# Mixture of experts: fp32 weights cast to bf16 by GpSimd's operations, and by transfers that GpSimd issues

## The chip, the cores and the metric

The kernel runs on one core of a Trainium2 chip. The metric is the device time of one execution in microseconds; the figure given for a kernel is the median of its runs. One further execution is recorded by the hardware profiler, and all rows below are from that one.

## The reference

A decoder of four layers over a tensor `x` of 4 x 256 tokens with 256 channels. Each layer adds an attention-like block, a cross block and a feed-forward block. The change lies in the feed-forward block of the first layer, a mixture of 64 experts of which each token uses 8:

```
router_logits = x2d @ gate_w                       # 1024 x 64
routing_weights, selected = top_k(softmax(router_logits), 8)
routing_weights /= sum(routing_weights)
layer_w0 = ragged_dot(x_bf16, gate_proj_bf16)      # expert e: 256 x 96
layer_w1 = ragged_dot(x_bf16, up_proj_bf16)        # expert e: 256 x 96
expert_out = ragged_dot(silu(layer_w0) * layer_w1, down_proj_bf16)   # 96 x 256
out = sum over the 8 experts of routing_weight * expert_out, to bf16
```

The weights come in as fp32 (`gate_proj`, `up_proj`, `down_proj`) and are rounded to bf16 before the products.

## The kernel before

The whole decoder is one program of stages, one after the other, each ended by a barrier of all engines. The function `mixture` (L1099) is the stage at hand. It computes every expert for every token and multiplies by the routing weight, which is 0 where the expert was not chosen.

**Units of weights.** An expert has only 96 inner columns, and the engines have 128 rows. The host packs four experts into three units of 128: unit r of a group holds the 96 columns of expert r and 32 columns of the fourth expert. So there are U = 48 units (`MOE_N`) for 64 experts. A unit has an up part (`moe_up[i]`, 128 x 512 fp32, gate and up weights, 256 KB) and a down part (`moe_down[i]`, 128 x 256 fp32, 128 KB). I call the work of one group, three units and four experts, a turn; there are 16.

**Rings.** SP loads unit i into slot i % 6 of the fp32 rings `wf` and `df` (L1161, L1162; `MOE_RING` = 6) and waits before it for the cast of unit i - 6. The two transfers of a unit raise one semaphore `loads[i % 6]`. GpSimd (`cast_weights`, from L1166) waits for both, and then copies `wf` into the bf16 ring `wb` (6 slots, L1172) and `df` into the bf16 ring `db` (9 slots, L1173). Before it writes it waits until the slots are free: for `wb` until TensorE has done the up product of unit i - 6 (`u_done`), for `db` until the down products of the group that used the slot are done (`o_done`). This last wait is the same for the three units of a group, so the casts come in bursts of three units. GpSimd also clears the accumulator `acc` once (L1178), after the casts of the first two units.

**The other engines, by unit i.** TensorE computes the gate and the up product of unit i for 1024 tokens into PSUM (`pg`, `pu`, L1198), when unit i is cast and the previous contents were read, and then the down products of the experts completed by unit i - 3 (`po`, L1213, `LAG` = 3). ScalarE copies `pg` to bf16 (L1229), computes the sigmoid from exponentials and a logarithm (L1232, L1247, L1249), and copies each expert's output from PSUM into `eo` (L1240). VectorE copies `pu` (L1297), adds 1 to the exponential (L1300), adds each expert's output times its routing weight into `acc` (L1308, eight instructions of 128 x 256 for an expert), and multiplies (L1318, L1324). After units 2, 5, 8, ... of a group the fourth expert is complete too, so VectorE then has two experts in a row: 16 instructions of L1308. At the start VectorE also computes the routing (L1266 to L1287) in three parts between the first units; TensorE's router products (L1186) come ahead of its first unit.

**Order.** Each engine's instructions run in the order written; between engines there are only the semaphores named. SP has nothing in this stage but the loads.

Of the kernel before, what the change touches and what calls it, by code (L numbers as in the profile page):

```python
# [15 lines left out]
BF16 = mybir.dt.bfloat16  # L16
# [4 lines left out]
P = 128  # L21
B = 4
S = 256
D = 256
KT = D // P
# [1066 lines left out]

MOE_E, MOE_F, MOE_N, MOE_RING = 64, 96, 48, 6
MOE_BIG = 2.0 ** 63


def mixture(nc, g):  # L1099


    res, xT, I = g["res"], g["xT"], g["in"]
    TOK = B * S
    with Stage(nc, "moe") as wst:
        acc = wst.sbuf("acc", [P, NT, D])
        wsel = wst.sbuf("wsel", [P, NT, MOE_E])
        xb = wst.sbuf("xb", [P, KT, TOK], BF16)
        wf = wst.sbuf("wf", [P, MOE_RING, KT, 2, P])
        df = wst.sbuf("df", [P, MOE_RING, D])
        gate = wst.sbuf("gate", [P, KT, MOE_E])  # L1110
        loads = [nc.alloc_semaphore(f"moe_loaded{r}", num=SEM_MOE + r) for r in range(MOE_RING)]
        normalize(nc, g, [(gate[:, :, :], I["moe_gate"])])

        with Stage(nc, "moee") as st:
            R, H, U, LAG = MOE_RING, 9, MOE_N, 3
            LAST = MOE_E - 1

            def before(i):

                return 4 * (i // 3) + i % 3  # L1120

            def experts(i):

                return range(before(i), before(i + 1))

            def pieces(e):

                n, r = 3 * (e // 4), e % 4
                return [(n + r, slice(0, MOE_F))] if r < 3 else [(n + i, slice(MOE_F, P)) for i in range(3)]

            wb = st.sbuf("wb", [P, R, KT, 2, P], BF16)
            db = st.sbuf("db", [P, H, D], BF16)
            gb = st.sbuf("gb", [P, 4, TOK], BF16)
            ub = st.sbuf("ub", [P, 4, TOK], BF16)
            ex = st.sbuf("ex", [P, 4, TOK], BF16)
# [11 lines left out]
            pl = po[:, 0:2, :].rearrange("p a (t e) -> p (a t) e", e=MOE_E)  # L1147
            logits, v_chain, shifted, prob_done, xb_done, zeroed = st.sem(
                "logits", "v_chain", "shifted", "prob_done", "xb_done", "zeroed")
            (cast, g_done, u_done, g_read, u_read, exp_done, one_plus, ln_done, inv_done, gated, h_done,  # L1150
             o_done, o_read, used, summed, rounded) = st.sem(
                "cast", "g_done", "u_done", "g_read", "u_read", "exp_done", "one_plus", "ln_done",
                "inv_done", "gated", "h_done", "o_done", "o_read", "used", "summed", "rounded")
            with st.block() as block:

                @block.sync
                def _(sp):
                    for i in range(U):
                        if i >= R:
                            sp.wait_ge(cast, i - R + 1)  # L1160
                        sp.dma_start(wf[:, i % R, :, :, :], I["moe_up"][i]).then_inc(loads[i % R], 16)  # L1161
                        sp.dma_start(df[:, i % R, :], I["moe_down"][i]).then_inc(loads[i % R], 16)  # L1162

                @block.gpsimd
                def _(pool):
                    def cast_weights(i):  # L1166
                        pool.wait_ge(loads[i % R], 32 * (i // R + 1))
                        if i >= R:
                            pool.wait_ge(u_done, i - R + 1)
                        if i >= H:  # L1170
                            pool.wait_ge(o_done, 4 * before(3 * ((i - H) // 3 + 1)))
                        nc.gpsimd.tensor_copy(wb[:, i % R, :, :, :], wf[:, i % R, :, :, :])  # L1172
                        nc.gpsimd.tensor_copy(db[:, i % H, :], df[:, i % R, :]).then_inc(cast, 1)  # L1173

                    AHEAD = 2
                    for i in range(AHEAD):
                        cast_weights(i)
                    nc.gpsimd.memset(acc[:, :, :], 0.0).then_inc(zeroed, 1)  # L1178
                    for i in range(AHEAD, U):
                        cast_weights(i)  # L1180

                @block.tensor
                def _(pe):
                    for t in range(NT):
                        for k in range(KT):
                            last = nc.tensor.matmul(pl[:, t, :], xT[:, k, t // ST, (t % ST) * P:(t % ST + 1) * P],  # L1186
                                                    gate[:, k, :], start=(k == 0), stop=(k == KT - 1))
                    last.then_inc(logits, 1)
                    pe.wait_ge(xb_done, KT)
                    for i in range(U + LAG):  # L1190
                        if i < U:
                            pe.wait_ge(cast, i + 1)
                            for n, (ps, read, done) in enumerate(((pg, g_read, g_done), (pu, u_read, u_done))):
                                if i >= 1:
                                    pe.wait_ge(read, i)
                                for half in range(2):
                                    for k in range(KT):
                                        last = nc.tensor.matmul(  # L1198
                                            ps[:, half, :], wb[:, i % R, k, n, :],
                                            xb[:, k, half * 512:(half + 1) * 512], start=(k == 0), stop=(k == KT - 1))  # L1200
                                last.then_inc(done, 1)
                        if i >= LAG:
                            pe.wait_ge(h_done, i - LAG + 1)
                            for e in experts(i - LAG):
                                for q in range(4):
                                    if e >= 1:
                                        pe.wait_ge(o_read, 4 * (e - 1) + q + 1)
                                    elif q == 0:
                                        pe.wait_ge(shifted, 1)
                                    for t in range(2 * q, 2 * q + 2):  # L1210
                                        parts = pieces(e)
                                        for n, (j, rows) in enumerate(parts):
                                            last = nc.tensor.matmul(  # L1213
                                                po[:, t, :], hb[rows, j % H, t * P:(t + 1) * P], db[rows, j % H, :],
                                                start=(n == 0), stop=(n == len(parts) - 1))
                                    last.then_inc(o_done, 1)
# [336 lines left out]
def attend(nc, g, name, H, HD, NKV, causal, scale, qparts, kparts, stacks, vaug, w_out, b_out, carried):  # L1553
# [12 lines left out]
    LAG = H + 12  # L1566
    AHEAD = 1 if H > 16 else 2
    OUT_AT, TURN_AT, NORM_AT = 5, 8, 9
    MAX_AT, ROWS_AT, O_AT, PROJ_AT, ADD_AT = 1, 7, H + 6, H + 7, H + 8
    with Stage(nc, name) as st:  # L1570
# [37 lines left out]
        with st.block() as block:  # L1608
# [25 lines left out]
            def _(pe):  # L1634
# [62 lines left out]
                def turn_max(u):  # L1697
                    pe.wait_ge(maxed, (u + 1) * H)
                    if u > AHEAD:
                        pe.wait_ge(added, u - AHEAD)  # L1700
                    for t in range(ST):
# [3 lines left out]
                def turn_o(u):  # L1705
                    pe.wait_ge(norm, (u + 1) * NQ)
                    pe.wait_ge(m_taken, 5 * min(u + AHEAD, B - 1) + 1)
                    for k in range(KT):
# [1505 lines left out]
def mamba3_ends(nc, g, name, m, end, start):  # L3214
# [7 lines left out]
    with Stage(nc, name) as st:  # L3222
# [12 lines left out]
        with st.block() as block:  # L3235
# [104 lines left out]
            def _(sp):  # L3340
                if start is not None:
                    sp.wait_ge(split_done, 1)
                    for q in range(L3_G):
                        for n in range(3):
# [3 lines left out]
                            sp.dma_start(rowsL[at + 3:at + 4, :, :], cs[of, 3 + n, :]).then_inc(rows, 16)  # L3348
                    sp.wait_ge(rows, 16 * 6 * L3_G)
STAGES = {0: mamba2, 1: context_mix, 2: mixture, 3: causal_attention, 4: mamba1, 5: ternary, 6: rotary_attention,  # L3350
          7: quant_experts, 8: half_tokens_then_mamba3, 10: positional_cross, 11: top_experts}

# [191 lines left out]
```

## Time and profile before

| | us |
|---|---|
| median of 3 runs | 2356.59 |
| the runs | 2351.8 to 2361.63 |
| the profiled execution | 2362.07 |
| its span | 2360.2 |
| VectorE busy in the span | 1758.0 |
| GpSimd busy in the span | 577.1 |
| the stage's first instruction; the first one of the next stage | 530.9; 908.4 |

The page counts an engine as busy while an instruction of its own runs; instructions overlap a little, so busy time divided by the count is less than the mean duration of one. Times in a timeline are from the span's start. The median over the runs and the profiled execution are different executions. The mean granted clock of TensorE was 0.86 of full speed.

### The profile page before, as it was taken

What the parts mean: (1) busy time and instruction counts of PE and PEld (TensorE: products, weight loads), DVE (VectorE), ACT (ScalarE), POOL (GpSimd) and SP (SyncE); (2) the same over time, 40 slices, a digit from 0 to 9 for tenths busy, and PEclk for the clock granted to TensorE, in tenths of its full rate; (3) what the DMA queues carried; (4) which work ended last, traced back from release to release, by engine and by line L of the source; (5) the groups of instructions that cost most, each with busy time, mean ns of one, the idle gap of its engine ahead of it and who ended that gap; (6) DMA issues with size and microseconds to landing.
All of it is one profiled execution on the core that took longest, in us unless ns stands there. A gap on an engine that the chain in (4) does not pass through costs nothing. (4 is left out here: it accounts for less than half of the span.)

```text
span 2360.2 us, 34189 instructions
## 1 busy us (share of the span) xinstructions
PE 1928.7 (82%) x10881; PEld 1278.6 (54%) x10881; DVE 1758.0 (74%) x3859; ACT 1335.1 (57%) x2651; POOL 577.1 (24%) x777
## 2 busy tenths in 40 slices
PE   5999999967776675866867985689999999858978
PEld 3767677754333333644652543466767676723545
DVE  5999899968999998657977855576555555568734
ACT  5888888858888886355433565324242424253641
POOL 3676677712111101004621001200101010120000
PEclk8999999987777777785677897599999999977989
DMA  8222222203211103304203000140000000052010
GB/s 291 85 83 82 94 84 81 82 2 121 61 47 55 41 1 92 95 10 97 49 29 89 15 3 18 59 199 3 3 0 2 0 2 1 1 127 65 16 38 18
DMA packets 81921, 132.02 MB, mean 56 GB/s; under 512 B 11631, under 2 KB 61887, under 8 KB 79307
## 3 DMA queue, kind: packets, MB, share of 16 engines
q1 hardware_dynamic: 78496, 125.35, 17.0%
q0 software_dynamic: 1728, 4.22, 0.8%
q8 instruction: 78, 1.28, 0.2%
q14 instruction: 83, 0.68, 0.1%
q10 hardware_dynamic: 1536, 0.49, 0.1%
HBM read 118.25 MB, written 10.88 MB: 55 GB/s over the span
## 5 line engine op out<-in xcount | busy, mean ns | idle before, releaser
L1308 DVE SCALAR_TENSOR_TENSOR moe_acc<-moee_eo,moe_wsel,moe_acc 128x256 f32<-128x256 bf16 x512 | 225.9, 512 | 0.6
L902 POOL TENSOR_SCALAR l_dec<-l_cumR,l_cum 128x128 f32<-128x128 f32 x192 | 160.9, 847 | 3.7 <-DMA l_ec<-l_rows 3.7
L927 DVE SCALAR_TENSOR_TENSOR l_acc<-l_px,l0w_chan,l_acc 128x253 f32<-128x253 f32 (+2 forms) x288 | 136.4, 474 | 31.6 <-POOL l_acc L882 29.8
L1240 ACT CAST moee_eo<-moee_po 128x512 bf16<-128x512 f32 x256 | 132.2, 597 | 38.1 <-PE moee_po L1213 34.8
L1198 PE MATMUL moee_pu<-moe_xb,moee_wb 128*128 128x512 bf16 x192 | 75.0, 533 | 88.4 <-DVE moee_ub L1297 88.4
L1213 PE MATMUL moee_po<-moee_db,moee_hb 96*128 96x256 bf16 (+1 forms) x768 | 128.8, 332 | 21.4 <-ACT moee_eo L1240 12.4
L1213 PEld LDWEIGHTS moee_po<-moee_db,moee_hb 96*128 96x128 bf16 (+1 forms) x768 | 88.9, 118 | 70.0 <-ACT moee_eo L1240 17.7
L1752 ACT ACTIVATE l3xa_ex<-l3xa_pS 128x512 f32<-128x512 f32 x128 | 74.0, 605 | 83.2 <-PE l3xa_pS L1665 78.8
L1752 ACT ACTIVATE l2a_ex<-l2a_pS 128x512 f32<-128x512 f32 x128 | 73.9, 605 | 78.6 <-PE l2a_pS L1665 74.1
L580 PE MATMUL l_pz<-xT,l0w_w_in 128*128 128x256 f32 x384 | 111.5, 414 | 0.0
L3168 POOL TENSOR_TENSOR l3w_yz<-l3b_ys,l3b_sz 128x256 f32<-128x256 f32 x48 | 40.2, 837 | 290.8 <-DVE l3b_ys L3197 290.8
L1172 POOL CAST moee_wb<-moe_wf 128x512 bf16<-128x512 f32 x48 | 37.6, 782 | 291.8 <-PE moee_po L1213 240.4
L3146 ACT COPY l3b_bc<-l3b_pbc 128x512 f32<-128x512 f32 x48 | 28.1, 586 | 137.2 <-PE l3b_pbc L3096 137.2
L967 DVE TENSOR_TENSOR l_gg<-l_dec,l_m 128x768 f32<-128x768 f32 x96 | 103.0, 1072 | 0.2
L580 PE MATMUL l_px<-xT,l0w_w_in 128*128 128x256 f32 x384 | 101.6, 387 | 0.7 <-DVE l_acc L927 0.7
L674 PE MATMUL l_po<-l0w_w_out,l_yg 128*128 128x256 f32 x384 | 100.8, 386 | 0.0
L1783 DVE TENSOR_REDUCE l3xa_negm<-l3xa_pA 128x2 f32<-128x512 f32 x128 | 83.2, 684 | 22.9 <-PE l3xa_pA L1649 21.1
L3096 PE MATMUL l3b_pbc<-l3w_xin,l3w_w_in 128*128 128x256 f32 x384 | 95.7, 392 | 5.3 <-PEq L72 5.3
L1783 DVE TENSOR_REDUCE l2a_negm<-l2a_pA 128x2 f32<-128x512 f32 x128 | 83.4, 684 | 22.1 <-PE l2a_pA L1649 20.3
L363 PE MATMUL ln_pt<-ident,xn 128*128 128x128 f32 x176 | 39.9, 419 | 69.3 <-DVE xn L278 69.2
L1198 PEld LDWEIGHTS moee_pu<-moe_xb,moee_wb 128*128 128x128 bf16 x192 | 20.9, 123 | 135.9 <-DVE moee_ub L1297 107.9
L2197 POOL TENSOR_TENSOR m1b_dBu<-m1w_du,m1b_bc 128x1024 f32<-128x1024 f32 x32 | 74.7, 2357 | 66.8 <-DMA m1b_bc<-bc_rows 39.0
(610 smaller groups left out, 5476.5 us busy)
## 6 DMA issues: line engine op xcount, KB each, us to landing
l_cumR<-l_rows SPq DMA_DIRECT2D x48, 512.0 KB, 3.6
l_ec<-l_rows SPq DMA_DIRECT2D x96, 128.0 KB, 3.9
moe_wf<-in_moe_up SPq DMA_DIRECT2D x48, 256.0 KB, 3.1
l3w_w_in<-in_l_w_in SPq DMA_DIRECT2D x1, 8224.0 KB, 25.4
m1b_bc<-bc_rows SPq DMA_DIRECT2D x16, 512.0 KB, 6.4
moe_df<-in_moe_down SPq DMA_DIRECT2D x48, 128.0 KB, 3.3
l_qs<-parts_q SPq DMA_DIRECT2D x36, 128.0 KB
l0w_w_in<-in_l_w_in SPq DMA_DIRECT2D x2, 1536.0 KB, 13.0
```

The source lines that it names most:

```text
L580: last = nc.tensor.matmul(out, w_in[:, k, c0:c0 + w], xT[:, k, b, :], start=(k == 0), stop=(k == KT - 1))
L674: last = nc.tensor.matmul(po[:, t * D:(t + 1) * D], yg[:, u % RY, t * P:(t + 1) * P], w_out[:, j, :], start=(j == 0 and t == 0), stop=(j = ...
L902: last = nc.gpsimd.tensor_scalar(dec[:, u % 2, e, S:SC], cumR[:, slot, 2 * (u % CU) + e, P:S], cum[:, b % 2, 1, head:head + 1], 0.0, ALU.a ...
L927: nc.vector.scalar_tensor_tensor(out=a, in0=px[:, u % 2, 0:S - (L0_CONV - 1 - c)], scalar=w, in1=a, op0=ALU.mult, op1=ALU.add).then_inc(ta ...
L967: nc.vector.tensor_tensor(gg[:, :, :], dec[:, v % 2, :, :], m3[:, bv % 2, None, :].broadcast_to([P, 2, SC]), ALU.mult).then_inc(gg_done, 1)
L1198: last = nc.tensor.matmul(ps[:, half, :], wb[:, i % R, k, n, :], xb[:, k, half * 512:(half + 1) * 512], start=(k == 0), stop=(k == KT - 1))
L1213: last = nc.tensor.matmul(po[:, t, :], hb[rows, j % H, t * P:(t + 1) * P], db[rows, j % H, :], start=(n == 0), stop=(n == len(parts) - 1))
L1240: nc.scalar.copy(eo[:, e % 2, 2 * q:2 * q + 2, :], po[:, 2 * q:2 * q + 2, :]).then_inc(o_read, 1)
L1308: last = nc.vector.scalar_tensor_tensor(out=acc[:, t, :], in0=eo[:, e % 2, t, :], scalar=wsel[:, t, e:e + 1], in1=acc[:, t, :], op0=ALU.mu ...
L1752: nc.scalar.activation(ex[:, at % XR, :, :], pS[:, at % 2, :, :], ACT.Exp, scale=scale).then_inc(exp_done, 1)
L1783: nc.vector.tensor_reduce(negm[:, u % 2, t, 2 * pair:2 * pair + 2], pA[:, at % 2, :, 0:keys(t)], AX, ALU.max, negate=True).then_inc(maxed, 1)
L3096: last = nc.tensor.matmul(pbc[:, n * S:(n + 1) * S], w_in[:, k, c0 + j * P:c0 + (j + 1) * P], xin[:, k, :], start=(k == 0), stop=(k == KT ...
```

## The change

SP's loads, the fp32 rings, the casts and the semaphore `cast` go. `wb` and `db` are now allocated in the outer stage. GpSimd issues, for each unit, a DMA from the fp32 weights straight into the bf16 ring `wb`, and another into `db`; such a transfer changes the type on its way. It waits before each for what the cast waited for. It clears `acc` before all loads. TensorE waits for the unit's load instead of for its cast.

```diff
-MOE_E, MOE_F, MOE_N, MOE_RING = 64, 96, 48, 6
+MOE_E, MOE_F, MOE_N, MOE_RING, MOE_DOWN = 64, 96, 48, 6, 9
...
-        wf = wst.sbuf("wf", [P, MOE_RING, KT, 2, P])
-        df = wst.sbuf("df", [P, MOE_RING, D])
+        wb = wst.sbuf("wb", [P, MOE_RING, KT, 2, P], BF16)
+        db = wst.sbuf("db", [P, MOE_DOWN, D], BF16)
...
-            R, H, U, LAG = MOE_RING, 9, MOE_N, 3
+            R, H, U, LAG = MOE_RING, MOE_DOWN, MOE_N, 3
...
-            wb = st.sbuf("wb", [P, R, KT, 2, P], BF16)
-            db = st.sbuf("db", [P, H, D], BF16)
...
-                @block.sync
-                def _(sp):
-                    for i in range(U):
-                        if i >= R:
-                            sp.wait_ge(cast, i - R + 1)
-                        sp.dma_start(wf[:, i % R, :, :, :], I["moe_up"][i]).then_inc(loads[i % R], 16)
-                        sp.dma_start(df[:, i % R, :], I["moe_down"][i]).then_inc(loads[i % R], 16)
-
                 @block.gpsimd
                 def _(pool):
-                    def cast_weights(i):
-                        pool.wait_ge(loads[i % R], 32 * (i // R + 1))
+                    def load(i):
                         if i >= R:
                             pool.wait_ge(u_done, i - R + 1)
+                        nc.gpsimd.dma_start(wb[:, i % R, :, :, :], I["moe_up"][i]).then_inc(loads[i % R], 16)
                         if i >= H:
                             pool.wait_ge(o_done, 4 * before(3 * ((i - H) // 3 + 1)))
-                        nc.gpsimd.tensor_copy(wb[:, i % R, :, :, :], wf[:, i % R, :, :, :])
-                        nc.gpsimd.tensor_copy(db[:, i % H, :], df[:, i % R, :]).then_inc(cast, 1)
-
-                    AHEAD = 2
-                    for i in range(AHEAD):
-                        cast_weights(i)
+                        nc.gpsimd.dma_start(db[:, i % H, :], I["moe_down"][i]).then_inc(loads[i % R], 16)
+
                     nc.gpsimd.memset(acc[:, :, :], 0.0).then_inc(zeroed, 1)
-                    for i in range(AHEAD, U):
-                        cast_weights(i)
+                    for i in range(U):
+                        load(i)
...
-                            pe.wait_ge(cast, i + 1)
+                            pe.wait_ge(loads[i % R], 32 * (i // R + 1))
```

## Rows read from the trace of the kernel before

**Rows 1.** The page's 40 slices: busy tenths of VectorE, each slice 59 us.
```profile
DVE  5999899968999998657977855576555555568734
```

**Rows 2.** Busy time by stretch: length, each engine's busy time, TensorE clock, DMA share, GB/s.
```profile
600.78:623.44 22.66, 15.26 (x72) 7.88 (x72) 22.52 (x46) 20.63 (x30) 3.81 (x6) 0.73 0.18 54
848.95:870.13 21.18, 15.84 (x72) 8.35 (x72) 21.04 (x46) 17.48 (x26) 0.00 (x0) 0.76 0.00 1
...
800.00:850.00 50.00, 32.41 (x147) 16.62 (x148) 49.69 (x98) 44.10 (x61) 7.85 (x12) 0.75 0.01 2
```

**Rows 3.** VectorE's L1308, grouped and alone, and L1300: ns min/median/max.
```profile
L1308 DVE SCALAR_TENSOR_TENSOR moe_acc<-moee_eo,moe_wsel,moe_acc 128x256 f32<-128x256 bf16 x512 | 225.9, 512 | 0.6
...
L1308 DVE SCALAR_TENSOR_TENSOR moe_acc<-moee_eo,moe_wsel,moe_acc x512: 471/479/832, 556.1 to 904.0; 128x256 f32<-128x256 bf16 x171
...
L1300 DVE TENSOR_SCALAR moee_ex<-moee_ex x48: 415/417/535, 543.0 to 882.0; 128x1024 bf16<-128x1024 bf16 x48
```

**Rows 4.** GpSimd's groups of the stage: busy us, mean ns, idle before.
```profile
L1172 POOL CAST moee_wb<-moe_wf 128x512 bf16<-128x512 f32 x48 | 37.6, 782 | 291.8 <-PE moee_po L1213 240.4 <-DMA moe_df<-in_moe_down 47.2 <-PE moee_pu L1198 4.1
L1173 POOL CAST moee_db<-moe_df 128x256 bf16<-128x256 f32 x48 | 26.7, 556 | 0.0
...
L1178 POOL MEMSET moe_acc<- 128x2048 f32 x1 | 1.8, 1807 | 0.0
```

**Rows 5.** VectorE's timeline, runs of 16 at L1308: start, length in us.
```profile
613.04 8.02 DVE L1308 SCALAR_TENSOR_TENSOR moe_acc<-moee_eo,moe_wsel,moe_acc 128x256 f32<-128x256 bf16 x16
...
635.70 7.89 DVE L1308 SCALAR_TENSOR_TENSOR moe_acc<-moee_eo,moe_wsel,moe_acc 128x256 f32<-128x256 bf16 x16
...
771.23 7.51 DVE L1308 SCALAR_TENSOR_TENSOR moe_acc<-moee_eo,moe_wsel,moe_acc 128x256 f32<-128x256 bf16 x16
...
838.56 8.01 DVE L1308 SCALAR_TENSOR_TENSOR moe_acc<-moee_eo,moe_wsel,moe_acc 128x256 f32<-128x256 bf16 x16
...
861.21 6.54 DVE L1308 SCALAR_TENSOR_TENSOR moe_acc<-moee_eo,moe_wsel,moe_acc 128x256 f32<-128x256 bf16 x16
```

**Rows 6.** GpSimd's timeline: first casts of two bursts, last cast of the stage.
```profile
570.65 1.07 POOL L1172 CAST moee_wb<-moe_wf 128x512 bf16<-128x512 f32 x1 [19.42 <-PE moee_po L1213]
...
612.89 0.70 POOL L1172 CAST moee_wb<-moe_wf 128x512 bf16<-128x512 f32 x1 [17.53 <-PE moee_po L1213]
...
841.63 0.59 POOL L1173 CAST moee_db<-moe_df 128x256 bf16<-128x256 f32 x1
```

**Rows 7.** Timeline of the stage's start, and TensorE's first product of unit 9.
```profile
530.92 7.06 PE L1186 MATMUL moee_po<-moe_gate,xT 128*128 128x64 f32 x32 [1.26 <-PEq L72]
...
535.81 0.61 POOL L1172 CAST moee_wb<-moe_wf 128x512 bf16<-128x512 f32 x1 [47.23 <-DMA moe_df<-in_moe_down]
...
539.48 1.91 PE L1198 MATMUL moee_pu<-moe_xb,moee_wb 128*128 128x512 bf16 x4
...
541.88 1.22 DVE L1297 CAST moee_ub<-moee_pu 128x1024 bf16<-128x1024 f32 x1
...
591.24 1.89 PE L1198 MATMUL moee_pg<-moe_xb,moee_wb 128*128 128x512 bf16 x4
```

**Rows 8.** Software DMAs: duration ns, us to landing; packets from 930 us, hardware from 525.
```profile
L1352 POOL DMA_DIRECT2D l_qs<-parts_q x12: 500/543/795, 935.5 to 1265.1; - x12
...
l_ks<-parts_k POOLq DMA_DIRECT2D x6, 128.0 KB, 4.2
...
l3x_ks<-parts_k POOLq DMA_DIRECT2D x6, 128.0 KB, 8.6
...
q0 software_dynamic: 576, 1.57, 28.5%
...
q1 hardware_dynamic: 4320, 5.90, 51.4%
```

**Rows 9.** Timeline of a later stage: the same VectorE operation without and beside them.
```profile
932.85 0.69 DVE L1511 TENSOR_TENSOR l1p_rest<-l1p_qf,l_pieces 128x512 f32<-128x512 f32 x1
...
935.53 3.11 POOL L1352 DMA_DIRECT2D l_qs<-parts_q  x6 [12.94 <-DMA parts_k<-l_pieces]
...
938.00 0.69 DVE L1511 TENSOR_TENSOR l1p_rest<-l1p_qf,l_pieces 128x512 f32<-128x512 f32 x1
```

More of the change, by code:

```diff
@@ L1149, in mixture @@
                 "logits", "v_chain", "shifted", "prob_done", "xb_done", "zeroed")
-            (cast, g_done, u_done, g_read, u_read, exp_done, one_plus, ln_done, inv_done, gated, h_done,
+            (g_done, u_done, g_read, u_read, exp_done, one_plus, ln_done, inv_done, gated, h_done,
              o_done, o_read, used, summed, rounded) = st.sem(
-                "cast", "g_done", "u_done", "g_read", "u_read", "exp_done", "one_plus", "ln_done",
+                "g_done", "u_done", "g_read", "u_read", "exp_done", "one_plus", "ln_done",
                 "inv_done", "gated", "h_done", "o_done", "o_read", "used", "summed", "rounded")
             with st.block() as block:
-                @block.sync
-                def _(sp):
-                    for i in range(U):
-                        if i >= R:
-                            sp.wait_ge(cast, i - R + 1)
-                        sp.dma_start(wf[:, i % R, :, :, :], I["moe_up"][i]).then_inc(loads[i % R], 16)
-                        sp.dma_start(df[:, i % R, :], I["moe_down"][i]).then_inc(loads[i % R], 16)
                 @block.gpsimd
                 def _(pool):
-                    def cast_weights(i):
-                        pool.wait_ge(loads[i % R], 32 * (i // R + 1))
+                    def load(i):
                         if i >= R:
                             pool.wait_ge(u_done, i - R + 1)
+                        nc.gpsimd.dma_start(wb[:, i % R, :, :, :], I["moe_up"][i]).then_inc(loads[i % R], 16)
                         if i >= H:
                             pool.wait_ge(o_done, 4 * before(3 * ((i - H) // 3 + 1)))
-                        nc.gpsimd.tensor_copy(wb[:, i % R, :, :, :], wf[:, i % R, :, :, :])
-                        nc.gpsimd.tensor_copy(db[:, i % H, :], df[:, i % R, :]).then_inc(cast, 1)
-                    AHEAD = 2
-                    for i in range(AHEAD):
-                        cast_weights(i)
+                        nc.gpsimd.dma_start(db[:, i % H, :], I["moe_down"][i]).then_inc(loads[i % R], 16)
                     nc.gpsimd.memset(acc[:, :, :], 0.0).then_inc(zeroed, 1)
-                    for i in range(AHEAD, U):
-                        cast_weights(i)
+                    for i in range(U):
+                        load(i)
                 @block.tensor
```

## The prediction

> **What bounds the kernel now.** Read the page's 40 slices first: the mixture of experts lies between 531 and 907 us, and there VectorE is busy at nine tenths in slice after slice [rows 1]. Then take the busy time of each engine over one turn of the work, three units of weights with four experts: in 22.66 us VectorE is busy 22.52 and ScalarE, the next, 20.63; TensorE is at 15.26 [rows 2]. Nothing but VectorE's own instruction stream sets this stage's length, so the change is worth what it takes off that stream, less what it makes VectorE wait for. GpSimd's casts, 37.6 + 26.7 = 64.3 us, are no bound themselves: GpSimd idles 291.8 us before them [rows 4]. The groups by line then show something odd: L1308, the add of an expert's output into the accumulator, always the same shape, has a mean of 512 ns against a median of 479 and a minimum of 471 [rows 3]. The timeline says where the mean comes from. L1308 comes in runs of 16 (two experts) once a turn; there are 15 such runs, and the first 13 take 7.89 us (seven), 8.02 (four), 8.01 (one) and 7.51 (one), the last two 6.54 each [rows 5]. The casts of a turn come in a burst that starts within such a run: 612.89 lies 0.15 us before the run at 613.04 and its six casts fill the next 3.8 us; the 13 bursts stand beside the 13 long runs, and after the last cast at 841.63 the runs are short [rows 5, 6]. That it is the casts and not the transfers is seen from 800 to 850 us: the loads are over, the DMA engines are busy 0.01 of the time and move 2 GB/s, yet the run at 838.56, which has casts, still takes 8.01 [rows 2, 5].
>
> **The change, part by part, against the profiled execution (2362.07 us, span 2360.2).**
>
> *Casts removed.* Excess over 6.54: 7 x 1.35 + 4 x 1.48 + 1.47 + 0.97 = 17.8 us, all inside VectorE's unbroken stream. One burst also met the 0.42 us operation of L1300 (maximum 535 ns, median 417): 0.1 us [rows 3]. The casts of the first nine units run beside the routing, on which I count nothing. Gain 17.9 us. Could another engine be late in its place? The turn without casts exists already: 848.95 to 870.13, 21.18 us, VectorE busy 21.04, ScalarE 17.48, TensorE 15.84 [rows 2]. So the whole 1.5 us of a turn comes back, and VectorE is still the bound after it. From below, 0 if something unseen takes the place; from above 17.9, since no other VectorE instruction here is longer than its minimum.
>
> *Generation of descriptors added on GpSimd.* 96 DMAs: 18 at the start, 78 in 13 bursts of about six (one may come earlier, its wait being only on u_done). The trace of before has software DMAs, issued from GpSimd at L1352: 500/543/795 ns [rows 8]. Their 6 in 3.11 us lie beside VectorE operations with two SBUF inputs; such an operation takes 0.69 us there and 0.69 us with GpSimd quiet, just before [rows 9]. So the generation takes nothing from VectorE: 0, by the nearest rows. But these DMAs have 576 packets for 12, 48 each, while the weights have 4320 for 30, 144 each [rows 8]. If the time went with the packets it would be 1.6 us for each and some 10 us for a burst, still less than half a turn of 22 us, and GpSimd does nothing else. Bounds: 0, and 78 x 0.54 = 42 us if VectorE stood still for each of them (rival A).
>
> *Steady state of the transfers.* A burst is released by the same wait (o_done of the group whose buffers it fills) and the weights are first read much later: released at 570.65, unit 9 is read by TensorE at 591.24 [rows 6, 7]. That is 20.6 us for a pair of 384 KB, and the later two of the burst have more. The reading of fp32 from memory stays the same (384 KB a unit), the write halves. A software transfer of 128 KB lands in 4.2 us beside others, in 8.6 in the slowest row [rows 8]. The lead covers both: 0. SP now issues nothing in this stage; nothing of the next stage was queued behind it, and the next stage's own loads start after its barrier as before. GpSimd's new waits (u_done, o_done) hold only further loads, nothing else is queued there.
>
> *The start.* Here there is no lead. Before, the first cast starts at 535.81, when the first pair has landed, and TensorE's first product waits not for it but for the router's products, 530.92 + 7.06 = 537.98; the second half ends at 539.48 + 1.91 = 541.39 and VectorE takes it at 541.88, busy until then: 0.49 us to spare [rows 7]. So the first pair must land by about 537.8 + 0.5 = 538.3. After: GpSimd starts with the stage at 530.9, clears acc (1.81 us, moved ahead of everything) [rows 4], generates the first transfer for 0.54, starts the second at 533.3, and with 4.2 us to land it is there at 537.5: hidden. With the longer generation (1.6 us each) the second starts at 534.3, ends its issue 1.1 us later than the short one would, and lands at 539.6: 1.3 us late. With 8.6 us on top of the later start: 542.9, 4.6 us late. I take 0.5 us, near the short end: the row of 4.2 us is from DMAs that share the engines with others, as these will, and the one of 8.6 us waited behind them longest. From the second unit on VectorE's routing leaves TensorE several us.
>
> *Memory.* 12 + 6 KB of fp32 rings go, 6 + 4.5 KB of bf16 take their place in the outer stage: no time. TensorE waits on the load's semaphore instead of a cast's: no time.
>
> **Sum.** -17.9 + 0.5 = -17.4: the profiled execution would come to 2362.07 - 17.4 = 2344.7 us. It stands 5.5 us above the median of the three runs; from the median, 2356.6 - 17.4 = **2339 us**. The change in the span is what I trust; the runs before spread over 9.8 us.
>
> A rule that speaks against the change: the Trainium skill's page "SBUF — State Buffer", section "Who interferes with whom", says that GpSimd shares a port pair with VectorE as a lock, and that software descriptor generation contends with VectorE's two-port modes, so that hardware-issued transfers are to be preferred. This case's rows show two-input operations unharmed beside software DMAs; L1300, which has a single SBUF source and 2-byte types, is the operation here to which the rule would apply, and rival B is that case.
>
> **Rivals.**
>
> A, on the slower side: *VectorE stands still while descriptors are generated.* The bursts fall just where the casts fell, in the runs of L1308, because the same o_done releases them. For: L1308 is slowed by GpSimd today, 1.4 us for 4 us of casts. Against: rows 9, where nothing is slowed. Price: 78 x 0.54 = 42 us, less 17.9: +24, 2381 us. It decides from 17.9 / 78 = 0.23 us lost per DMA; below that the change still gains. Chance 0.06.
>
> B: *the generation holds up L1300 alone.* It can be hit once a turn at most, as its neighbours are short: 13 x 0.54 = 7 us, 2346 us; with 1.6 us generations 13 x 1.6 = 21 and the gain is gone. Against: 0.42 us of every 6, and the bursts begin in the run after it, in 12 of 13 turns. The Trainium skill's lock rule, named above, would give this time; no row here decides it. Chance 0.08.
>
> C: *casting transfers are slow.* No row shows a transfer that changes the type. A turn of 22 us takes three pairs, so nothing is lost below 7 us a pair and everything above: at 9 us, 48 x 9 = 432 us for the loads against a stage of 376, +56, 2413 us. Slower, too. Against: 384 KB in 7 us is 55 GB/s, where the first loads, 5.90 MB in 51.4% of 35 us, came at 328 [rows 8]. Chance 0.05.
>
> D: *the start is late in full*, 4.6 us instead of 0.5: 2343 us. Chance 0.07.
>
> E: *nothing comes back*, because what lengthens L1308 is the pairing of the two experts and the casts only mark the time: 2357 us. Against: the two short runs of 16. Chance 0.04.
>
> **How the numbers follow.** The forecast has 0.70, its own range 2333 to 2346 (start 0 to 1.3, and about 5 us of spread between medians of a few runs); B and D lie in or near it. 0.5% is 11.8 us, about what can be told from no change here. Faster by more: nearly all of the forecast (0.66) and most of D and half of B, 0.74. Within: the rest of these and E, 0.16. Slower: A and C, with B's long form, 0.10. The range for 8 in 10 is 2331 to 2352: it takes in B's short form and D and leaves A and C out.
>
> **What would show it.** Right: all 15 runs of L1308 at 6.54 us and its mean near 480 ns; turns of 21.2 us throughout; VectorE idle in the stage still below 1 us; GpSimd with 96 DMAs and one memset; software packets up by some 13,800, those of the first hardware queue down by as many; ub's first cast at 541.9 to 542.4. Wrong: runs of L1308 above 7 us beside GpSimd's DMAs (A), L1300 above 0.5 us (B), TensorE waiting for moe_up or moe_down after the first unit (C), a first ub at 546 (D).

## The result, and the profile after

| | before | after |
|---|---|---|
| median, us (20 runs each, same chip) | 2360.09 | 2355.03 |
| lowest to highest | 2351.8 to 2368.92 | 2347.08 to 2359.24 |
| the profiled execution; its span | 2362.07; 2360.2 | 2353.93; 2352.0 |
| VectorE busy in the span | 1758.0 | 1741.0 |

The ratio is 0.998 (95% interval 0.9971 to 0.9988): the change saves 4.7 us, 2.8 to 6.8. The sign was forecast and the size was not: 17.4 us were predicted, and 2339 us with a range of 2331 to 2352; 2355 lies outside it. In the two profiled executions the mixture, from the router's first product to the end of the last L1294 (L1308 before), shrank from 373.6 to 370.3 us, by 3.3; the other 4.9 us between the spans lie outside it, where the code is the same.

First the page's VectorE slices (40 equal ones, busy tenths), then its DMA queues (packets, bytes in MB, time as a share), both to be held against [rows 1, 8].

```profile
DVE  5999899968999997757978856576555555568734
...
q1 hardware_dynamic: 64672, 106.47, 14.4%
q0 software_dynamic: 15552, 13.66, 4.1%
```

The slices don't show what is new: nine tenths through the stage, as before, since 1.1 us of new idling in 22 doesn't change a digit. The software queue gained 15552 - 1728 = 13824 packets, and the first hardware queue lost as many (78496 before): the change does what it says. Now the groups by line of the stage after the change (busy us, mean ns of one, idle time just before them and what ended it). L1294 is L1308 of before and L1286 is L1300 [rows 3]; L1304, the multiply by the gate, was L1318.

```profile
L1294 DVE SCALAR_TENSOR_TENSOR moe_acc<-moee_eo,moe_wsel,moe_acc 128x256 f32<-128x256 bf16 x512 | 208.0, 478 | 0.6
L1304 DVE TENSOR_TENSOR moee_gb<-moee_gb,moee_ex 128x1024 bf16<-128x1024 bf16 x48 | 33.2, 691 | 13.4 <-ACT moee_ex L1235 13.2
L1286 DVE TENSOR_SCALAR moee_ex<-moee_ex 128x1024 bf16<-128x1024 bf16 x48 | 20.0, 417 | 0.0
L1162 POOL DMA_DIRECT2D moe_db<-in_moe_down x48 | 26.5, 552 | 235.8 <-PE moee_po L1199 235.7
L1159 POOL DMA_DIRECT2D moe_wb<-in_moe_up x48 | 26.4, 551 | 21.4 <-PE moee_pu L1184 21.4
```

L1294 gave back exactly what was counted: 225.9 - 208.0 = 17.9 us. But a wait of 13.4 us stands in the second row, and before there was none: VectorE now waits for ScalarE's exponential. The view of waits (who waits on whom: us in all, times, the longest) gives it thirteen times, after 13 of the 15 runs of 16, and shows what ScalarE itself waits for:

```profile
DVE moee_gb L1304 <- ACT moee_ex L1235: 13.2, 13, 1.1
...
ACT moee_eo L1226 <- PE moee_po L1199: 32.3, 48, 0.8
```

By the windows over the stage, VectorE's busy time fell by 16.7 us (363.16 to 346.49: the 17.9 less small differences elsewhere) and its idle time rose by 13.4, which leaves the 3.3. The same by the time line: the start is 0.4 us shorter, the 14 turns between the 15 runs of 16 take 310.24 us instead of 314.39 (4.15 less), and the end, which holds one of the thirteen waits, is 1.2 longer.

The place of the wait is the turn's middle. This is the timeline of one turn after the change (start, length, engine, line; idle time before it in brackets):

```profile
587.14 2.70 ACT L1226 CAST moee_eo<-moee_po 128x512 bf16<-128x512 f32 x5
587.76 5.24 PE L1199 MATMUL moee_po<-moe_db,moee_hb 32*128 32x256 bf16 x24 [2.71 <-ACT moee_eo L1226]
588.08 6.54 DVE L1294 SCALAR_TENSOR_TENSOR moe_acc<-moee_eo,moe_wsel,moe_acc 128x256 f32<-128x256 bf16 x16
590.48 0.59 ACT L1226 CAST moee_eo<-moee_po 128x512 bf16<-128x512 f32 x1 [0.64 <-PE moee_po L1199]
591.76 0.59 ACT L1226 CAST moee_eo<-moee_po 128x512 bf16<-128x512 f32 x1 [0.69 <-PE moee_po L1199]
593.04 0.59 ACT L1226 CAST moee_eo<-moee_po 128x512 bf16<-128x512 f32 x1 [0.69 <-PE moee_po L1199]
593.30 0.53 POOL L1162 DMA_DIRECT2D moe_db<-in_moe_down  x1 [18.32 <-PE moee_po L1199]
593.52 1.06 ACT L1233 ACTIVATE moee_lx<-moee_ex 128x1024 f32<-128x1024 bf16 x1
594.61 1.06 ACT L1235 ACTIVATE moee_ex<-moee_lx 128x1024 bf16<-128x1024 f32 x1
595.70 0.69 DVE L1304 TENSOR_TENSOR moee_gb<-moee_gb,moee_ex 128x1024 bf16<-128x1024 bf16 x1 [1.08 <-ACT moee_ex L1235]
```

VectorE's run of 16 is short, 6.54 us, and done at 594.62. Its multiply needs the exponential of the same unit. ScalarE writes it last of all: first it copies the fourth expert out of PSUM, a quarter at a time, and waits 0.64 + 0.69 + 0.69 = 2.0 us for TensorE's 24 products on 32 rows, here called the chain. The chain starts only 0.3 us before VectorE's run and takes 5.24 us; copy, logarithm and exponential end at 595.67. Before the change the chain began mostly 3.1 us ahead of the run (its lead; only at the first run was it as short as 1.0), and the run was longer. Two such chains of the kernel before (their runs of 16 start at 613.04 and 861.21):

```profile
609.94 2.79 PE L1213 MATMUL moee_po<-moee_db,moee_hb 32*128 32x256 bf16 x24 [1.14 <-ACT moee_eo L1240]
858.11 4.50 PE L1213 MATMUL moee_po<-moee_db,moee_hb 32*128 32x256 bf16 x24 [1.14 <-ACT moee_eo L1240]
```

Last, busy time by stretch for the kernel after: two of its turns, then a stretch at TensorE's pause and the start of the next chain. The columns are those of [rows 2].

```profile
588.08:610.44 22.36, 16.00 (x74) 8.65 (x72) 21.14 (x45) 20.06 (x29) 3.18 (x6) 0.73 0.23 27
854.28:876.61 22.33, 16.01 (x73) 8.65 (x72) 21.15 (x46) 20.06 (x29) 0.00 (x0) 0.73 0.00 0
605.00:608.00 3.00, 1.19 (x10) 0.72 (x8) 3.00 (x8) 2.97 (x5) 0.00 (x0) 1.00 0.00 0
609.00:611.00 2.00, 0.88 (x5) 0.61 (x6) 2.00 (x5) 2.00 (x5) 0.00 (x0) 0.50 0.01 4
```

These turns are 22.3 to 22.4 us with transfers and without, VectorE busy 21.15 of it: 1.1 of the 1.2 us missing are its wait. ScalarE is busy 20.06 and waits some 2 us for the chain, so ScalarE with its waits now fills the turn as well. TensorE pauses before each chain for a free buffer. In the pause of 3.94 us before the chain at 610.12 its granted clock (the clock that the throttle grants it) is at 1.00 (2.4 GHz) up to 608, and from 609 on at 0.50 (1.2 GHz), where the whole chain runs. The chain at 609.94 of before ran in 2.79 us at full clock:

```profile
609.94:612.70 2.76, 2.76 (x25) 2.19 (x26) 2.73 (x4) 2.76 (x6) 0.00 (x0) 1.00 0.02 6
```

But not every turn of the kernel after is like that. Of its 14 turns ten take 22.33 to 22.42 us, and four take 21.36, 21.43, 21.69 and 21.71. The last of these is the first turn, whose chain led by 1.0 us. The other three begin with the three chains that ran partly at full clock. Here are one of those and the chain after it, each followed by the multiply that needs it; the last two rows are TensorE's busy time and granted clock over the two chains:

```profile
654.97 4.23 PE L1199 MATMUL moee_po<-moe_db,moee_hb 32*128 32x256 bf16 x24 [2.39 <-ACT moee_eo L1226]
661.90 0.69 DVE L1304 TENSOR_TENSOR moee_gb<-moee_gb,moee_ex 128x1024 bf16<-128x1024 bf16 x1
676.33 5.30 PE L1199 MATMUL moee_po<-moe_db,moee_hb 32*128 32x256 bf16 x24 [2.25 <-ACT moee_eo L1226]
684.32 0.69 DVE L1304 TENSOR_TENSOR moee_gb<-moee_gb,moee_ex 128x1024 bf16<-128x1024 bf16 x1 [1.14 <-ACT moee_ex L1235]
...
654.97:659.20 4.23, 4.23 (x25) 0.64 0.00 0
676.33:681.63 5.30, 5.30 (x25) 0.50 0.00 0
```

The same 24 products, the same lead of 0.31 us, the same VectorE operations: with the clock at 0.64 on the average the chain is 1.07 us shorter, VectorE doesn't wait, and the turn takes 21.36 us instead of 22.42. The chain of 832.53 (4.30 us, clock 0.63) left no wait either, the one of 788.42 (4.56 us, 0.59) left 0.40 us. So within one kernel the wait follows the length of the chain, and that length the granted clock.

### The profile page after: what moved, and what is told of

Same layout as the page of the kernel before. It is cut to its first block and busy times, and to the rows that moved or that the text cites. A ratio compares the mean times of both kernels' runs of the same rounds, so it can differ in the third digit from the quotient of the medians.

```text
span 2352.0 us, 34051 instructions
## 1 busy us (share of the span) xinstructions
PE 1946.4 (83%) x10881; PEld 1287.6 (55%) x10881; DVE 1741.0 (74%) x3859; ACT 1336.0 (57%) x2651; POOL 567.2 (24%) x777
## 3 DMA queue, kind: packets, MB, share of 16 engines
q0 software_dynamic: 15552, 13.66, 4.1%
## 5 line engine op out<-in xcount | busy, mean ns | idle before, releaser
L1294 DVE SCALAR_TENSOR_TENSOR moe_acc<-moee_eo,moe_wsel,moe_acc 128x256 f32<-128x256 bf16 x512 | 208.0, 478 | 0.6
L1199 PE MATMUL moee_po<-moe_db,moee_hb 96*128 96x256 bf16 (+1 forms) x768 | 146.3, 364 | 47.5 <-ACT moee_eo L1226 42.6
L1199 PEld LDWEIGHTS moee_po<-moe_db,moee_hb 96*128 96x128 bf16 (+1 forms) x768 | 97.3, 129 | 104.3 <-ACT moee_eo L1226 48.3
L1769 DVE TENSOR_REDUCE l3xa_negm<-l3xa_pA 128x2 f32<-128x512 f32 x128 | 83.3, 684 | 22.4 <-PE l3xa_pA L1635 20.6
L1184 PE MATMUL moee_pg<-moe_xb,moe_wb 128*128 128x512 bf16 x192 | 66.2, 480 | 32.9 <-ACT moee_gb L1215 32.9
L2172 ACT ACTIVATE m1b_dA<-m1w_delta,m1w_a 128x255 f32<-128x255 f32 x128 | 53.3, 462 | 62.3 <-DVE m1b_h L2195 59.9
L755 ACT ACTIVATE l_dec<-l_cumR,l_cum 128x256 f32<-128x256 f32 x192 | 87.5, 508 | 0.4 <-DMA l_ec<-l_rows 0.4
```

Source lines behind the costliest of these rows:

```text
L755: last = nc.scalar.activation(dec[:, u % 2, e, 0:S], row, ACT.Relu, bias=cum[:, b % 2, 0, head:head + 1])
L1199: last = nc.tensor.matmul(po[:, t, :], hb[rows, j % H, t * P:(t + 1) * P], db[rows, j % H, :], start=(n == 0), stop=(n == len(parts) - 1))
L1294: last = nc.vector.scalar_tensor_tensor(out=acc[:, t, :], in0=eo[:, e % 2, t, :], scalar=wsel[:, t, e:e + 1], in1=acc[:, t, :], op0=ALU.mu ...
L1769: nc.vector.tensor_reduce(negm[:, u % 2, t, 2 * pair:2 * pair + 2], pA[:, at % 2, :, 0:keys(t)], AX, ALU.max, negate=True).then_inc(maxed, 1)
```

## The experiments

Each kernel was timed in turn with the kernel before on the same chip; the ratios are to that one. A ratio can differ by some 0.1% from the quotient of the two medians, which is 3 us here, so where a gain is compared both are given.

**e1: is the new wait the work of what was added?** The kernel before, where the casts stop after the first nine units, so that the later products use old weights and the output is wrong. No software transfers.

```diff
-                        if i >= R:
+                        if R <= i < R + H:
                             sp.wait_ge(cast, i - R + 1)
+                        elif i >= R + H:
+                            sp.wait_ge(u_done, i - R + 1)
...
-                    for i in range(AHEAD, U):
+                    for i in range(AHEAD, H):
                         cast_weights(i)
...
-                            pe.wait_ge(cast, i + 1)
+                            if i < H:
+                                pe.wait_ge(cast, i + 1)
+                            else:
+                                pe.wait_ge(loads[i % R], 32 * (i // R + 1))
```

> The kernel before, but GpSimd casts only the first nine units: later units are loaded as fp32 by SP as before and never cast, so TensorE computes with the first units' weights. No casts in the steady state and no software DMAs. Theory (the chain): with the casts gone the turn is bound by ScalarE's instructions plus its waits for the fourth expert's 24 products at TensorE's lower clock; then this kernel is like the changed one: 5 us under before (2355), runs of 16 at L1313 or so of 6.54 us, turns of 22.4 us and about 13 us of VectorE idle before the multiply by the sigmoid. Rival (what was added): the idle comes from the software DMAs or their generation; then the turns are 21.2 us, no idle, and the time is 17 us under before (2343).

Measured: 2356.32 us beside 2359.08, ratio 0.9997 (0.9981 to 1.0013). The stage's groups of this kernel (L1313 is the add into the accumulator, L1323 the multiply):

```profile
L1313 DVE SCALAR_TENSOR_TENSOR moe_acc<-moee_eo,moe_wsel,moe_acc 128x256 f32<-128x256 bf16 x512 | 208.0, 478 | 0.6
L1323 DVE TENSOR_TENSOR moee_gb<-moee_gb,moee_ex 128x1024 bf16<-128x1024 bf16 x48 | 33.2, 691 | 11.7 <-ACT moee_ex L1254 11.6
```

The same short operations and the same wait, without one of the new DMAs. The wait comes with the removal of the casts; nothing that was added makes it. The time can't be told from that of the kernel before: by the interval at most 4.5 us were saved, where 5 were expected and 17 by the rival. In the trace its 14 turns take 308.4 us, 6.0 less than before. The chains show again what was seen above: after those of 4.15, 4.29 and 4.41 us the turn takes 21.3 to 21.6 us, after those of 5.2 to 5.3 us 22.3 to 22.4 (the second run's excepted, whose chain led by 1.5).

**e2 and e3: is it the chain?** The fourth expert's products cut from 24 to 8, in the kernel after (e2) and in the one before (e3); two thirds of that expert's output are left out.

```diff
-... else [(n + i, slice(MOE_F, P)) for i in range(3)]
+... else [(n + i, slice(MOE_F, P)) for i in range(2, 3)]
```

> The changed kernel with the fourth expert's 24 down products of a turn cut to 8 (one of its three pieces; its output lacks two thirds of that expert). Theory: the chain of products, 5.3 us at the lower clock, is what ScalarE waits for, so with 1.8 us in its place VectorE's idle before the multiply goes from 13 us to under 2, the turns fall to 21.2 us and the time to 2342 (13 us under the changed one, 18 under before). Rival (what was added): no difference, 2355.

> The kernel before with the same cut of the fourth expert's products. Theory: VectorE was never idle there, the casts' delay covered the chain, so the cut is worth nothing: 2360, within 2 us, turns of 22.5 to 22.7 us, runs of 16 still 7.9 us. Rival (TensorE or ScalarE shares the bound already before): 3 to 10 us faster.

Measured: e2 2340.00 us beside 2359.08, 0.9914 (0.9883 to 0.9944); e3 2354.55 us, 0.998 (0.9965 to 0.9995). The multiply and one turn of e2:

```profile
L1304 DVE TENSOR_TENSOR moee_gb<-moee_gb,moee_ex 128x1024 bf16<-128x1024 bf16 x48 | 32.9, 684 | 0.0
...
629.88:651.05 21.17, 14.18 (x54) 6.22 (x54) 21.03 (x45) 18.98 (x28) 2.17 (x5) 0.66 0.21 26
```

With a short chain the wait is gone, the turn is the 21.17 us that I had read as the general case, and between e3 and e2 the change is worth 14.5 us by the medians, 15.6 by the ratios. e3 missed its expectation: it came out 4.5 us under the unchanged kernel (1.2 to 8.3 by the interval) where none was expected, within the band set down for its rival, that TensorE or ScalarE shares the bound already before. The trace speaks for another cause: VectorE waits before no multiply, but with the shorter chain the casts start earlier (at 676.48, say, 1.2 us ahead of the run at 677.63, where they started within the run or 0.15 us before it), 11 of its 13 long runs are 7.51 us instead of 7.9 to 8.0, and L1308 takes 220.7 us in all instead of 225.9, 5.2 less.

**e4, e5, e9: is it ScalarE's order?** The chain stays whole. ScalarE computes the logarithm after its first quarter copy of the fourth expert and the exponential after the second, where it would wait for TensorE anyway. e4 and e9 are this edit in the kernel after, e5 in the one before.

```diff
                                     nc.scalar.copy(eo[:, e % 2, 2 * q:2 * q + 2, :],
                                                    po[:, 2 * q:2 * q + 2, :]).then_inc(o_read, 1)
+                                    if e % 4 == 3 and i <= U:
+                                        if q == 0:
+                                            log_part(i - 1)
+                                        if q == 1:
+                                            exp_part(i - 1)
-                        if 1 <= i <= U:
-                            ...
+                        if 1 <= i <= U and not (i >= LAG and i % 3 == 2):
+                            log_part(i - 1)
+                            exp_part(i - 1)
```

> The changed kernel with ScalarE's logarithm and second exponential of the previous unit placed between its copies of the fourth expert's quarters (after the first and after the second), where it idles 0.69 us three times a turn for TensorE. Theory: the multiply finds its factor ready; what is left is up to 0.3 us a turn by which the later quarters come late to VectorE: 2343 to 2347, idle before the multiply near 0. Rival (what was added): 2355.

> The kernel before with ScalarE's reordering of the fourth expert's iteration, casts kept. Theory: VectorE is bound by its own stream lengthened by the casts, so nothing to gain: 2360 within 2 us. If the reordering by itself is worth 10 us or more here, the recovery in the changed kernel would not speak for the chain.

> The changed kernel with ScalarE's reordering once more, beside the changed kernel on the same chip: 2345, 10 us under it, 14 under before. If the earlier run was luck, it lies within 3 us of the changed one.

Measured: e4 2344.56 us beside 2359.08, 0.9952 (0.9931 to 0.9972); e5 2358.13 beside 2360.00, 0.9998 (0.9978 to 1.0017); e9 2345.67 beside 2360.43, 0.9946 (0.9933 to 0.9959). First the timeline of e4 in the middle of a turn, then two groups (L1294 is here the copy of `pu`, L1315 the multiply):

```profile
631.77 5.30 PE L1199 MATMUL moee_po<-moe_db,moee_hb 32*128 32x256 bf16 x24 [3.90 <-ACT moee_eo L1238]
...
633.80 1.06 ACT L1214 ACTIVATE moee_lx<-moee_ex 128x1024 f32<-128x1024 bf16 x1
...
635.22 1.07 ACT L1218 ACTIVATE moee_ex<-moee_lx 128x1024 bf16<-128x1024 f32 x1
...
638.57 0.69 DVE L1315 TENSOR_TENSOR moee_gb<-moee_gb,moee_ex 128x1024 bf16<-128x1024 bf16 x1
...
L1294 DVE CAST moee_ub<-moee_pu 128x1024 bf16<-128x1024 f32 x48 | 58.5, 1219 | 4.3 <-PE moee_pu L1184 4.2
...
L1315 DVE TENSOR_TENSOR moee_gb<-moee_gb,moee_ex 128x1024 bf16<-128x1024 bf16 x48 | 32.9, 685 | 0.0
```

The chain is as long as ever (5.30 us), but the exponential is ready at 636.29, 2.3 us before VectorE comes to it. The wait is gone, and 4.3 us of it return as a wait for TensorE's up product. In the kernel before the same edit gives nothing that can be told from none: there VectorE did not wait. With ScalarE in this order the removal of the casts is worth 2358.13 - 2344.56 = 13.6 us by the medians, which are from two chips, and 10.9 by the ratios, instead of 4.7. The kernel after with this order is the fastest complete version: by the medians 14.5 and 14.8 us under the one before, by the ratios 11 and 13. Beside e8 below, the kernel after on the same chip, e9 is 11.1 us faster by the medians and 8.7 by the ratios.

**e6, e7: do the casts hide the wait?** The kernel after, which also makes the casts, from a scratch tile into another, for every unit from the tenth on. In e6 a unit's two casts follow its two DMAs; in e7 the six of a burst come back to back and the DMAs behind them. This is e7's edit, without the new tiles and their clearing.

```diff
                         if i >= H:
                             pool.wait_ge(o_done, 4 * before(3 * ((i - H) // 3 + 1)))
+                        if i >= H and i % 3 == 0:
+                            for n in range(3):
+                                pool.wait_ge(scratch, 2 + 2 * (i - H + n))
+                                nc.gpsimd.tensor_copy(wz[:, :, :, :], wf[:, :, :, :]).then_inc(scratch, 1)
+                                nc.gpsimd.tensor_copy(dz[:, :], df[:, :]).then_inc(scratch, 1)
                         nc.gpsimd.dma_start(db[:, i % H, :], I["moe_down"][i]).then_inc(loads[i % R], 16)
```

> The changed kernel, in which GpSimd also makes, for units 9 and later, the two casts of a unit as before, from scratch memory into scratch memory, each pair after the unit's DMAs. Theory: the casts take 1.4 us of a run of 16 and cost the time only 4 to 5 us, because VectorE's idle before the multiply (13 us) disappears: 2359 to 2362. Rival (the casts' cost and the new idle are separate): both are there, 2355 + 18 = 2373.

> The changed kernel with the six casts of three units made back to back by GpSimd, scratch to scratch, when the group's down slots come free, as in the kernel before; its DMAs follow. In the run before, where each pair of casts stood between DMAs, a run of 16 took 9.25 us and the time rose by 17 us over the changed kernel. Theory: in one burst the casts take 1.4 us of a run as they did, the chain's idle covers 1.1 of it, and the time is 2359 to 2362, 4 to 6 us above the changed kernel, with no idle before the multiply. Rival (casts cost their full price beside software DMAs, whatever their order): 2372.

> The changed kernel itself, on the same chip as the two others of this job: 2355, 0.2% under before.

Measured: e6 2371.83 us beside 2360.00, 1.0057 (1.0033 to 1.0082); e7 2357.26 beside 2360.43, 0.9994 (0.9977 to 1.0012); e8, the kernel after once more on the chip of e7 and e9, 2356.80, 0.9983 (0.9971 to 0.9995). A run of 16 of e6 with GpSimd's casts inside it, and its multiply:

```profile
616.29 9.26 DVE L1305 SCALAR_TENSOR_TENSOR moe_acc<-moee_eo,moe_wsel,moe_acc 128x256 f32<-128x256 bf16 x16
...
618.40 0.62 POOL L1169 CAST moe_wz<-moe_wf 128x512 bf16<-128x512 f32 x1
620.34 0.63 POOL L1169 CAST moe_wz<-moe_wf 128x512 bf16<-128x512 f32 x1
...
623.06 0.62 POOL L1170 CAST moe_dz<-moe_df 128x256 bf16<-128x256 f32 x1
...
L1315 DVE TENSOR_TENSOR moee_gb<-moee_gb,moee_ex 128x1024 bf16<-128x1024 bf16 x48 | 33.1, 689 | 0.0
```

The same of e7, and one of its chains:

```profile
611.37 8.06 DVE L1306 SCALAR_TENSOR_TENSOR moe_acc<-moee_eo,moe_wsel,moe_acc 128x256 f32<-128x256 bf16 x16
...
615.04 0.62 POOL L1169 CAST moe_wz<-moe_wf 128x512 bf16<-128x512 f32 x1 [15.40 <-PE moee_po L1211]
...
L1316 DVE TENSOR_TENSOR moee_gb<-moee_gb,moee_ex 128x1024 bf16<-128x1024 bf16 x48 | 33.1, 689 | 0.0
...
857.20 2.79 PE L1211 MATMUL moee_po<-moe_db,moee_hb 32*128 32x256 bf16 x24 [1.14 <-ACT moee_eo L1238]
```

e7 shows the other direction: with the casts back, the runs are 7.9 to 8.1 us again and VectorE's wait goes from 13.4 us to 0.0, while the time is the same as e8's within what can be told; it was expected 2 to 5 us higher. The casts cost 18 us and hid some 13. Its first four chains still took 5.3 us and left no wait, so the longer run alone is enough to hide them. Turn by turn the chain's lead then grows, from 1.0, 1.4 and 1.7 us at the first three runs to 3.1, and chains of 2.79 us are there again. e8's trace repeats the wait of the kernel after: 13.3 us. e6 missed its expectation by about 10 us: the same six casts, spread between DMAs, lengthen a run by 2.7 us and not by 1.4, more than the wait that they hide. Its time is close to the rival's 2373, but not for the rival's reason, which had the wait stay: it is 0.0.

## Why the prediction was wrong in size

**What held.** *Casts removed*: all 15 runs of 16 take 6.54 us and L1294 falls by 17.9 us, the term as worked out. *Generation of descriptors*: 96 DMAs at 551 and 552 ns, 0.53 in the timeline row; with three times the packets of [rows 8] they take no longer, so the 1.6 us did not come, and with all runs at 6.54 us neither did rival A. L1286 stays at 417 ns, so rival B's time did not come either; but in this trace no DMA is being issued while an L1286 runs (at 596.82 the last of a burst, until 597.35, and L1286 at 598.17), so what such a meeting would cost stays open. *Steady state of the transfers*: they land in 3.4 us (up, 256 KB read) and 2.8 (down, 128 KB read), medians, and no product after the first unit waits for them; rival C is out. *The start*, set at +0.5, came out at nothing, and D with it: the rows of after (gap before the clearing, the first DMA, the first product, the first copy of `pu`) are

```profile
529.66 1.81 POOL L1164 MEMSET moe_acc<- 128x2048 f32 x1 [42.03 <-POOLq L72]
531.41 0.81 POOL L1159 DMA_DIRECT2D moe_wb<-in_moe_up  x1
...
536.56 1.91 PE L1184 MATMUL moee_pg<-moe_xb,moe_wb 128*128 128x512 bf16 x4
...
540.60 1.22 DVE L1283 CAST moee_ub<-moee_pu 128x1024 bf16<-128x1024 f32 x1
```

From the stage's begin to that copy it is 10.9 us, as it was in [rows 7].

**What failed.** The step is "Could another engine be late in its place?", answered with "the whole 1.5 us of a turn comes back, and VectorE is still the bound after it". It is off by 13.4 us of VectorE waiting for ScalarE. Two readings went wrong in it.

The first: the turn of 848.95 to 870.13 was taken as "the turn without casts". It is one, but the first after thirteen turns with casts, and its chain had a lead of 3.1 us. With that lead even its slow chain (858.11, 4.50 us) did no harm: ScalarE's exponential was ready at 865.28, 2.5 us before the run's end at 867.75. Nor did the slowest chain of the kernel before, which took about 5.3 us, from 655.5 to 660.8, with the clock at 0.50 and a lead of 2.7 us: there the exponential was ready at 663.56, and the run at 658.22 would have ended at 664.76 even without casts. By these rows the wait takes both, a long chain and a short lead. In the kernel after, where no turn has casts, the lead is 1.0 us at the first run and 0.3 at every later one, and the turn at the same place takes 22.33 us (the window of 854.28 above); e1 has the same wait with nothing added. That the casts build up the lead is seen in e7. How many turns a lead of 3.1 us would last without casts no run shows: e7's one such turn, 860.30 to 881.48, still ended with all of it, after a chain of 2.79 us.

The second: ScalarE was set down at 17.48 us of 21.18. That window held 26 of its instructions, where the turn's other row has 30 and 20.63 us [rows 2]; the stretch was cut from VectorE's side, so ScalarE's share of a turn fell partly outside it. From 861.21 to 882.38, the next 21.17 us without casts, ScalarE has 29 instructions and 20.13 us. And busy time was compared alone. Here is the view of waits of ScalarE in those two stretches of the kernel before, 600.78 to 623.44 first, then 848.95 to 870.13:

```profile
ACT moee_eo L1240 <- PE moee_po L1213: 1.4, 1, 1.4
ACT moee_eo L1240 <- DVE moe_acc L1308: 0.4, 1, 0.4
```

```profile
ACT moee_eo L1240 <- PE moee_po L1213: 3.5, 3, 2.1
```

20.63 + 1.8 = 22.4 of 22.66 us, and 17.48 + 3.5 = 21.0 of 21.18. With its waits ScalarE was as full as VectorE in the very rows on which the step stood. That alone doesn't make it a bound, since a wait can be slack too, but it forbids calling it free. What the change then gave back was 0.1 to 0.2 us for the usual turn (22.52 to 22.66 before, 22.42 after) and 0.3 on the average of the 14, not 1.5. TensorE's clock, which sets the length of the chain, stands in no term of the prediction, though the chains of before already ranged from 2.79 to 5.3 us.

**What the runs settle, and what they don't.** That the wait comes from the removal alone (e1), passes through the chain (e2) and through ScalarE's order (e4, e9), and is hidden again by casts (e7), is shown by runs. That the granted clock makes the chain long or short is read from the traces, not set by an experiment: the same products take 2.79 us with the clock at 1.00, 4.23 at 0.64 and 5.24 to 5.30 at about 0.50, and inside the kernel after, the wait and the length of the turn go with it. e2 shortened the chain by its products, not by its clock. Why the clock is lower in some chains than in others stays open: in the kernel before, the chains of 2.79 and of 4.50 us both follow a pause of 1.14, and the one of 5.3 us at 0.50 follows none. A kernel that keeps TensorE busy through its pause was not tried.

## What to carry to other kernels

Before crediting time taken off the busiest engine, add each other engine's waits on third engines to its busy time, over a full turn that holds all its instructions: only what that leaves of the turn is sure to be won. A stretch at the end of a loop that already lacks the cost is no safe preview, since it starts with a lead that the other engines may owe to the cost; compare that lead, and ask how many turns in a row have run without it. A group whose length varies from turn to turn with the same instructions, like the chain here, is worth a look at the granted clock. And where a second engine takes over as the bound, look at what it does while it waits: here two instructions moved into its gaps, with no effect in the kernel before that could be told from none, raised the gain from 4.7 us to 11 to 15.

## What the hardware did that I had not expected

The same six GpSimd casts, 3.5 to 3.8 us of work, cost VectorE's run of 16 1.4 to 1.5 us when they come back to back (e7, 8.06 against 6.54 us) and 2.7 us when they are spaced by DMAs (e6, 9.26). Mean L1294 time is 478 ns without them, 515 and 543 with. Where the difference comes from is open. The Trainium skill's page "SBUF — State Buffer", section "Who interferes with whom", says that a VectorE instruction with two SBUF inputs contends with a GpSimd instruction that reads SBUF. The traces agree as to who is hit: the add with its two inputs is, and it is free when the casts go. The page doesn't tell the two spacings apart.

Issuing a software DMA took 0.54 us with 48 packets (the median in [rows 8]) and 0.55 with 144, and no add was longer for it: some 34 of the 96 were issued beside L1294, whose 512 instructions lie between 473 and 485 ns.
